# A DLRM tower on one Trainium2 core: all four groups of layer 1 in three rounded passes, and two of the 32 product banks of a chunk moved from VectorE to ScalarE

## The reference, cut to what matters

```
e = stack([tbl_f[ids[:, f]] for f in 32 fields])       # 512 samples x 32 fields x 32 numbers
prev, outs = e, []
for W in (filter_0, filter_1):                         # two layers of 128 maps
    z = einsum('bhd,bmd->bhmd', e, prev)               # every pair of a field and a previous map
    cur = relu(einsum('bpd,pn->bnd', z.reshape(b, h * m, d), W[0]))
    prev = cur
    outs.append(cur)
pooled = sum(concatenate(outs, axis=1), axis=-1)       # 512 x 256
h = relu(concatenate([pooled, dense_ctx], 1) @ W_top1 + b_top1)
h = relu(h @ W_top2 + b_top2)
y = h @ W_top3
```

## Time and profile before

| what | us |
|---|---|
| time before, median of 3 runs | 878.09 |
| lowest and highest of the three | 877.87, 881.36 |
| the profiled execution, its own time | 877.02 |
| its span, first to last instruction | 875.1 |
| TensorE busy | 855.4 (98%) |
| VectorE busy | 797.1 (91%) |
| ScalarE busy | 683.0 (78%) |
| GpSimd busy | 678.2 (77%) |

### The profile page before, as it was taken

How to read it: one execution, slowest core, us unless ns; L and a number is a source line. 1 busy time by engine, 2 the same in 40 slices (tenths; PEclk the granted TensorE clock), 3 DMA queues, 4 the chain that set the end, 5 groups by cost and what they waited for, 6 DMA issues and landing times.

```text
span 875.1 us, 17350 instructions
## 1 busy us (share of the span) xinstructions
PE 855.4 (98%) x3581; PEld 670.2 (77%) x3581; DVE 797.1 (91%) x2392; ACT 683.0 (78%) x2230; POOL 678.2 (77%) x676
## 2 busy tenths in 40 slices
PE   2999999999999999999999999999999999999998
PEld 2678777777877777787777787777778777778884
DVE  3799999999989999999999999999999998999884
ACT  2588787788888778888778888877888877888883
POOL 5278887879778797979878787887878888786781
DMA  6786666767756676665767656577675676773430
GB/s 184 227 205 144 156 153 140 182 158 158 174 116 156 152 182 157 151 163 109 176 157 177 163 134 156 126 174 166 162 178 116 138 163 165 160 181 76 86 72 1
DMA packets 55486, 131.21 MB, mean 150 GB/s; under 512 B 8101, under 2 KB 19333, under 8 KB 55462
## 3 DMA queue, kind: packets, MB, share of 16 engines
q0 software_dynamic: 22240, 68.17, 42.7%
q1 hardware_dynamic: 31538, 59.99, 21.2%
q10 hardware_dynamic: 1683, 2.80, 1.0%
HBM read 60.67 MB, written 4.20 MB: 74 GB/s over the span
## 4 chain that ended last, share of the span: by engine, by line
PE 95%; DMA 2%; DVE 1%; ACT 0%; POOL 0%; issue 0%; SPq 0%; DVEq 0%; ACTq 0%
PE t_act L721 14%; PE t_dve L721 13%; PE t_act L723 13%; PE t_act L722 13%; PE t_dve L723 13%; PE t_dve L722 13%; PE acc L689 6%; PE acc L694 5%; PE acc_pool L731 1%; PE acc L698 1%; PE acc_pool L733 1%; DMA x_shift<-x_rows 1%; PE acc L675 1%; DVE prod L554 0%; PE t_act L804 0%; POOL emb L249 0%
## 5 line engine op out<-in xcount | busy, mean ns | idle before, releaser
L395 ACT ACTIVATE prod<-t_act,weigh 128x128 f32<-128x128 f32 x2048 | 578.8, 373 | 115.4 <-PE t_act L723 113.6
L543 DVE SCALAR_TENSOR_TENSOR prod<-t_dve,weigh,prod 128x128 f32<-128x128 f32 x1792 | 480.8, 339 | 10.4 <-PE t_dve L723 6.7
L286 POOL TENSOR_TENSOR prod<-prod 128x512 f32<-128x512 f32 (+1 forms) x255 | 320.5, 1257 | 18.5 <-DMA prod<-prod 8.4
L721 PE MATMUL t_act<-w_hi,cur_hi 128*128 128x512 f32 x512 | 215.8, 422 | 0.1
L721 PE MATMUL t_dve<-w_hi,cur_hi 128*128 128x512 f32 x512 | 200.1, 391 | 0.0
L723 PE MATMUL t_act<-w_hi,cur_lo 128*128 128x512 f32 x512 | 199.9, 391 | 0.0
L722 PE MATMUL t_act<-w_lo,cur_hi 128*128 128x512 f32 x512 | 199.9, 390 | 0.0
L723 PE MATMUL t_dve<-w_hi,cur_lo 128*128 128x512 f32 x512 | 199.4, 389 | 0.0
L722 PE MATMUL t_dve<-w_lo,cur_hi 128*128 128x512 f32 x512 | 199.3, 389 | 0.0
L268 POOL DMA_DIRECT2D prod<-prod x126 | 118.5, 941 | 96.6 <-DVE prod L543 73.7
L249 POOL DMA_INDIRECT emb<-table_dram,all_ids x128 | 160.4, 1253 | 34.4 <-issue 23.2
(11 more groups left out here) (85 smaller groups left out, 580.7 us busy)
## 6 DMA issues: line engine op xcount, KB each, us to landing
prod<-prod POOLq DMA_DIRECT2D x126, 512.0 KB, 5.0
x_shift<-x_rows SPq DMA_DIRECT2D x64, 512.0 KB, 6.0
x_pair<-x_rows SPq DMA_DIRECT2D x96, 128.0 KB, 4.4
x_same<-x_rows SPq DMA_DIRECT2D x32, 256.0 KB, 3.4
x_rows<-emb SPq DMA_DIRECT2D x64, 64.0 KB
w_raw<-w_dram ACTq DMA_DIRECT2D x8, 256.0 KB, 5.1
emb<-table_dram,all_ids POOLq DMA_INDIRECT x128, 2.6
w_raw<-wt_dram SPq DMA_DIRECT2D x2, 512.0 KB, 4.7
```

The costliest lines, as they stand in the source:

```text
L286: nc.gpsimd.tensor_tensor(src[:, dst, :], src[:, dst, :], src[:, other, :], ALU.add).then_inc(folded, 1)
L395: last = nc.scalar.activation(prod[i][:, HEADS * k + j, :], t_act[k % ARING][:, j * MAPS:(j + 1) * MAPS], ACT.Copy, scale=weigh[p][:, i, h ...
L543: nc.vector.scalar_tensor_tensor(dst, src, w, dst, ALU.mult, ALU.add).then_inc(added, 1)
L721: nc.tensor.matmul(bank[:, :], cur_hi[p][:, cols], w_hi[:, w], start=True, stop=False)
```

## The change

1. `round_pair` and `lower_pair` are done for all four groups, in two halves (`which` 0 and 1); `z_hi`, `z_lo`, `v_hi` and `v_lo` are twice as large. From chunk 2 on, layer 1 takes three passes per group. Layer 1 of chunk 1 is now whole fp32 in all four groups. The first half's rounding of chunk c + 2 stands at the end of chunk c, on ScalarE behind tile 3, on VectorE behind the last `products`.
2. The banks of a tile are given out by a string: tiles 0 and 2 by `ADAADADA` (five to ScalarE, three to VectorE), tiles 1 and 3 by `ADADADAD` (four each, as before). ScalarE thus has 18 banks of a chunk and VectorE 14, where each had 16. The rings keep 2 and 4 banks. Where ScalarE has five banks, `prod[i]` has 20 slots, `halve` moves 10, and `fold` takes three steps (5, 2 and 1 slots wide) where it took two.
3. `place` goes from VectorE to ScalarE, behind tile 2. VectorE's transpose goes behind tile 0. GpSimd's `halve` goes ahead of the two gathers.
4. To make room in SBUF, the context operands of the top layer lie in `w_raw`, and `pool1_hi`/`pool1_lo` in `z_hi`/`z_lo`. The first matmuls of the top layer now all wait for all of VectorE's banks.

```
-                    n = tile * HALF + k // 2
-                    if k % 2 == 1:
-                        bank, done = t_dve[(k // 2) % DRING], dve_bank
+                    before_k = ORDER[i][:k].count(ORDER[i][k])
+                    if ORDER[i][k] == "D":
+                        n = c * D_CHUNK + D_BEFORE[i] + before_k
+                        bank, done = t_dve[(p * D_CHUNK + D_BEFORE[i] + before_k) % DRING], dve_bank
                         wait(pe, added, (n - DRING + 1) * HEADS)
                     else:
-                        bank, done = t_act[(k // 2) % ARING], act_bank
+                        n = c * A_CHUNK + A_BEFORE[i] + before_k
+                        bank, done = t_act[(A_BEFORE[i] + before_k) % ARING], act_bank
                         wait(pe, weighed, n - ARING + 1)
...
+ORDER = ["ADAADADA", "ADADADAD"] * (TILES // 2)
...
-            def round_pair(c, p):
-                act.wait_ge(z_ready, c * 3 + 3)
-                act.wait_ge(layer1_done, c)
-                nc.scalar.activation(z_hi[:, :, :], z[p][:, WHOLE:GROUPS, :], ACT.Copy).then_inc(pair_rounded, 1)
+            def round_pair(c, p, which):
+
+                g = slice(which * 2, which * 2 + 2)
+                act.wait_ge(z_ready, c * 3 + 1 + 2 * which)
+                act.wait_ge((layer1_half, layer1_done)[which], c - 1 + which)
+                nc.scalar.activation(z_hi[:, g, :], z[p][:, g, :], ACT.Copy).then_inc(pair_rounded, 1)
...
             def chunk(c, p):
                 for i in range(TILES):
                     weigh_tile(c, i, p)
-                    if i == 0 and not (isinstance(c, int) and c + 1 >= CHUNKS):
-                        round_pair(c + 1, 1 - p)
+                    if i == 0 and not (isinstance(c, int) and (c == 0 or c + 1 >= CHUNKS)):
+                        round_pair(c + 1, 1 - p, 1)
+                    if i == 2:
+                        place(c, p)
+                    if i == 3 and not (isinstance(c, int) and c + 2 >= CHUNKS):
+                        round_pair(c + 2, p, 0)
...
+                add_tile(c, 0, p)
                 if more1:
                     transpose(c + 1, 1 - p)
-                add_tile(c, 0, p)
-                if more1:
-                    lower_pair(c + 1, 1 - p)
-                place(c, p)
+                if more1 and not (fixed and c == 0):
+                    lower_pair(c + 1, 1 - p, 1)
                 add_tile(c, 1, p)
...
                 if more2:
                     products(c + 2, p, 1)
+                    lower_pair(c + 2, p, 0)
...
-                    if g < WHOLE:
-
-                        if g == 0:
-                            pe.wait_ge(z_ready, c * 3 + 1)
-                        nc.tensor.matmul(acc1[:, :], v[:, g, :], z[p][:, g, :], start=g == 0, stop=False)
...
                     elif g < GROUPS:
-                        k = g - WHOLE
-                        pe.wait_ge(z_lo_ready, (c - 1) * SPLIT + k + 1)
+                        pe.wait_ge(z_lo_ready, (c - 2) * GROUPS + g + 1)
...
-                pe.wait_ge(added, (CHUNKS * TILES * HALF - DRING + f + 1) * HEADS)
+                pe.wait_ge(added, CHUNKS * D_CHUNK * HEADS)
```

More of the change, by code:

```diff
@@ L15 @@
 GROUPS = 4
-SPLIT = 2
-WHOLE = GROUPS - SPLIT
+WHOLE = GROUPS // 2
 BANK = 512
@@ L22 @@
 BANKS = FIELDS // HEADS
-HALF = BANKS // 2
-FEEDS = HALF * HEADS
+ORDER = ["ADAADADA", "ADADADAD"] * (TILES // 2)
+A_BANKS, D_BANKS = ([order.count(who) for order in ORDER] for who in "AD")
+A_BEFORE, D_BEFORE = ([sum(banks[:i]) for i in range(TILES + 1)] for banks in (A_BANKS, D_BANKS))
+A_CHUNK, D_CHUNK = A_BEFORE[TILES], D_BEFORE[TILES]
 DRING, ARING = 4, 2
@@ L78, in dlrm_tower @@
         w_lo = sb("w_lo", [128, FIELDS * MAPS], f32r)
-        prod = [sb(f"prod{i}", [128, FEEDS, MAPS]) for i in range(TILES)]
+        prod = [sb(f"prod{i}", [128, A_BANKS[i] * HEADS, MAPS]) for i in range(TILES)]
         side = [sb(f"side{p}", [128, TILES, MAPS]) for p in range(2)]
@@ L272, in fold @@
             def fold(c, i, p, halve_here=False):
-                src = prod[i]
-                tile = c * TILES + i
-                done = tile * len(FOLDS)
+                src, half = prod[i], HALVES[i]
                 if halve_here:
-                    pool.wait_ge(weighed, (tile + 1) * HALF)
-                    pool.wait_ge(added, (tile + 1) * FEEDS)
+                    pool.wait_ge(weighed, c * A_CHUNK + A_BEFORE[i + 1])
+                    pool.wait_ge(added, (c * D_CHUNK + D_BEFORE[i + 1]) * HEADS)
                 else:
                     pool.wait_ge(halved[i % 2], (c * (TILES // 2) + i // 2 + 1) * 16)
-                for step, (dst, other) in enumerate([HALVE] * halve_here + FOLDS):
+                done = c * sum(len(FOLDS[h]) for h in HALVES) + sum(len(FOLDS[h]) for h in HALVES[:i])
+                steps = [(slice(0, half), slice(half, 2 * half))] * halve_here + FOLDS[half]
+                for step, (dst, other) in enumerate(steps):
                     if step > 0:
@@ L314, in chunk @@
                         halve(c, i)
+                    if ahead and i < 2:
+                        gather(c + LEAD, (2 * i, 2 * i + 1))
                     if i > 0:
@@ L389, in weigh_tile @@
                     act.wait_ge(weigh_ready, c + 1)
-                for k in range(HALF):
-                    act.wait_ge(act_bank, tile * HALF + k + 1)
+                banks = [k for k, who in enumerate(ORDER[i]) if who == "A"]
+                for a, k in enumerate(banks):
+                    n = A_BEFORE[i] + a
+                    act.wait_ge(act_bank, c * A_CHUNK + n + 1)
                     for j in range(HEADS):
-                        h = HEADS * 2 * k + j
-                        last = nc.scalar.activation(prod[i][:, HEADS * k + j, :],
-                                                    t_act[k % ARING][:, j * MAPS:(j + 1) * MAPS], ACT.Copy,
+                        h = HEADS * k + j
+                        last = nc.scalar.activation(prod[i][:, HEADS * a + j, :],
+                                                    t_act[n % ARING][:, j * MAPS:(j + 1) * MAPS], ACT.Copy,
                                                     scale=weigh[p][:, i, h:h + 1])
@@ L494, in products, with lower_pair @@
                                             ALU.mult).then_inc(z_ready, 1)
-            def lower_pair(c, p):
-                dve.wait_ge(pair_rounded, c)
-                for k in range(SPLIT):
-                    nc.vector.tensor_tensor(z_lo[:, k, :], z[p][:, WHOLE + k, :], z_hi[:, k, :].bitcast(fp32),
+            def lower_pair(c, p, which):
+                dve.wait_ge(pair_rounded, (c - 2) * 2 + which + 1)
+                for g in (which * 2, which * 2 + 1):
+                    nc.vector.tensor_tensor(z_lo[:, g, :], z[p][:, g, :], z_hi[:, g, :].bitcast(fp32),
                                             ALU.subtract).then_inc(z_lo_ready, 1)
```

92 lines of the change are left out of this document (50 added, 42 removed).

## The result

| | before | after |
|---|---|---|
| time, median of 4 runs | 878.05 us | 1024.73 us |
| lowest and highest | 877.87, 881.36 | 1024.40, 1024.78 |
| span of the profiled execution | 875.1 us | 1022.9 us |
| mean granted clock of TensorE | 1.000 | 0.953 |

The ratio is 1.165, with an interval of 1.162 to 1.168. The sign is the forecast one; the size is 147 us where 44 were forecast.

What follows compares the result with a forecast made beforehand. TensorE, busy 98%, was taken to bound the kernel. Per chunk, 1.89 us of stalls less 0.14 and 0.35 gave +1.40; with the ends, 44.8 us on 877.02, forecast 922 us, range 902 to 937.

Steps and rivals of the forecast that it cites:

- What else moves, costed at nothing in the loop: Work moved on VectorE and GpSimd costs nothing in the loop; VectorE has 2.3 us of cover before layer 1.
- tile 0, fourth bank: TensorE waits 0.29 us a chunk for ScalarE, which comes late from tile 3's last bank and the new rounding.
- tile 2, fourth bank: TensorE waits 0.50 us a chunk for ScalarE, whose `relu1` stands ahead of the tile's first bank.
- tile 3, its start: TensorE starts the tile 0.12 us late, waiting for ScalarE to free tile 2's sixth bank.
- tile 3, fifth bank: TensorE waits 0.98 us a chunk, as `place`, `relu2` and `round_last` stand ahead of ScalarE's first bank.
- stalls of the kernel before: TensorE's stall of 0.14 us a chunk for a ScalarE bank before the change, subtracted from the new stalls.
- three passes for fp32: In layer 1, two fp32 groups taking 1.71 us become six matmuls taking 1.36, saving TensorE 0.35 us a chunk.
- period: Length of one chunk in the loop: 25.77 us before, forecast 1.40 longer at 27.17.
- Rival 1: ScalarE's 4.7 us of idle time a chunk absorbs its 3.3 of new work; 863 us; chance 0.05.
- Rival 2: ScalarE's pile behind tile 2 is smaller, only 0.12 remaining of 0.98; chunk costs 0.54, time 895 us; chance 0.10.
- Rival 3: VectorE and GpSimd hinder each other; VectorE loses 3 us a chunk, TensorE waits 0.7; 944 us; chance 0.06.
- What would show it: Signs: TensorE busy 93 or 94%, four waits a chunk for ScalarE's `prod` near 60 us in all, period near 27.2.

Runs made afterwards that it cites:

- a_pad16: The changed kernel with 16 one-column memsets added in VectorE's prologue, ahead of its loop: 925.84 us, ratio 1.050 to the kernel before.
- a_head4: The changed kernel with VectorE's first four chunks written out instead of two: 925.67 us, ratio 1.049 to the kernel before.
- a_ring3: The changed kernel with VectorE's first four chunks written out and three banks for each ring instead of two and four: 904.04 us, ratio 1.027.
- a_place: The changed kernel with VectorE's first four chunks written out and the `place` copy back on VectorE: 924.32 us, ratio 1.048.
- b_head4: The kernel before, without the change, with VectorE's first four chunks written out instead of two: 910.36 us, ratio 1.032.

## Why the prediction was wrong, and where it was right

**The step that failed** is the part headed "What else moves, costed at nothing in the loop". It costed VectorE's lost instructions by their time alone ("VectorE loses two banks ... and `place`") and found cover enough. It never asked where the instructions themselves lie. The change shortened the code ahead of VectorE's loop by 20 instructions and the loop by 33, and with that the loop touches three blocks of 256 where it touched two. That costs TensorE some 7.7 us thirteen times, 100.6 us, 98% of the miss (16 instructions of padding take it away: a_pad16). No rival had it. The cover of 2.3 us that the step named was far too little for 9.6.

**The sum itself** held. Without the standstill (a_head4), in us a chunk:

| term | forecast | measured |
|---|---|---|
| tile 0, fourth bank | 0.29 | 0.20 + 0.10 = 0.30 |
| tile 2, fourth bank | 0.50 | 0.30 + 0.11 = 0.41 |
| tile 3, its start | 0.12 | 0.10 |
| tile 3, fifth bank | 0.98 | 0.73 + 0.11 = 0.84 |
| stalls of the kernel before | -0.14 | -0.14 |
| three passes for fp32 | -0.35 | -0.28 |
| period | 27.17 | 27.00 |

The -0.28 is what remains: 27.00 - 1.65 of stalls = 25.35, against 25.77 - 0.14 = 25.63. Two terms were a tenth too large. In tile 2 `relu1` came 0.20 after the tile's first matmul (510.60 - 510.40), not 0.29. In tile 3 the start's own 0.10 was counted twice: it lies behind the start of the first matmul (516.35 to 516.68) and so moves the fifth bank's due time too. The copy took 0.19 and not 0.26, and `relu2` and `round_last` 0.54 and 0.52 as forecast. The total of 921.3 has luck in it: thirty chunks at 0.17 less are 5 us less than forecast, and a_head4's chunk 1 lasts 30.48, 3.5 more than its others, since VectorE waits 7.1 us there for a transfer of `x_shift`, which I had not foreseen.

**The rivals.** Rival 1 (the spare time absorbs it) falls: the period is 27.0 and ScalarE still waits 57.9 us for TensorE in a_pad16, in the wrong places. Rival 2 falls by the 0.84. Rival 3 is real, but VectorE's ring of four banks covers it in a_head4; in a_ring3 it reaches TensorE. GpSimd's work was put at nothing too, and once in a_head4, six times in a_place, ScalarE waits for it. "What would show it" was met by the four stalls a chunk (73.1 us where near 60 were said) and not by TensorE's share, 88% instead of 93 or 94; in a_head4 it is 95%.

## What to carry to other kernels

A bank ring is judged by the distance from one use to the next against fill + read + release (here 2.16 us), at the place where side work stands ahead of a tile's first bank; put such work inside a tile, between banks, and remember that a bank given to one ring is taken from another. A change to a kernel with loops also changes where the code lies: when an engine waits for "issue" at the head of its loop, and the queue of instruction fetches has several packets for each jump, shift the loop (write out another pair, or pad) before judging the change. Count every instruction for that, waits and register instructions too, and confirm by a run.

## What the runs showed of the hardware

- A loop of 289 to 325 instructions on VectorE starts again 0.2 to 0.3 us behind its branch when it lies in two blocks of 256. In three blocks VectorE is idle 4.2 to 6.0 us a jump where the next edge lies 50 instructions behind the head (b_head4), and 8.6 to 10.3 us where it lies one behind it (the changed kernel), with five more fetches a jump (65 for 13). Each fetch is 0.68 MB / 83 = 8.2 kB.
- After a wait of 5.81 us TensorE's clock was at its 1.2 GHz level for about nine matmuls (seven to fifteen after the other waits of 4.65 to 6.81 us). In b_head4, where TensorE waits 1.85 to 2.79 us eleven times, the clock fell to that level behind three of them (2.54, 1.99 and 2.73 us) and stayed at 1.00 behind eight (1.85 to 2.79). The view by windows, for the stretch around the jump before the one above (us, busy PE, PEld, DVE, ACT, POOL, clock, DMA share, GB/s):

```profile
402.60:410.33 7.73, 6.91 (x23) 5.58 (x24) 7.73 (x28) 2.29 (x9) 3.74 (x4) 0.78 0.42 81
```

  The granted clock is 0.78 there and 1.00 in the chunks on both sides. So such a wait cost a third more than its length or more (1.88 beside 5.81 in the pair shown, 27.8 beside 72.5 in all).
- ScalarE's copy of 128x128 from SBUF to SBUF takes a step of 0.19 us (0.32 long), less than its 0.26 for the same tile from PSUM with a factor per partition.
